# Waiting only for counters that have moved: the entry waits of a fully serialised eight-core kernel

## What is computed

```python
def bit_linear(x, w):
    xn = (x - mu) / jnp.sqrt(var + 1e-05)              # over a whole batch element
    wq = jnp.clip(jnp.round(w * ws), -1.0, 1.0) / ws   # ternary weights
    xq = jnp.clip(jnp.round(xn * xs), -128.0, 127.0) / xs
    return xq @ wq.T

def ode_func(z, Wqkv, Wo_o, a_o, b_o):                 # called 8 times
    h = dyn_tanh(z, a_o, b_o)
    q, k, v = split(bit_linear(h, Wqkv))               # 16 heads of 64
    attn = softmax(q @ k.T * scale)
    return bit_linear(attn @ v, Wo_o)

xn = layernorm(x)
h = xn + retention(xn)
s = ode_block(h)                                       # 2 steps of 4 ode_func
g = silu(ffn(xn))                                      # 1024 -> 4096 -> 1024
return x + s * g
```

## Time and profile before

| | before |
|---|---|
| median of 3 runs | 43872.15 us (43852.11 to 43897.67) |
| profiled execution, its time | 43859.97 us |
| profiled execution, span of the slowest core | 43858.4 us |
| spans of the 8 cores | 43794.8 to 43858.4 us |
| mean granted TensorE clock, by core | 0.612 to 0.613 |
| instructions of the slowest core | 223059 |
| PE / DVE / ACT / POOL busy | 12665.3 / 7484.7 / 10799.9 / 834.4 us |

### The profile page before, as it was taken

The page is one execution under the profiler, slowest core; times in us unless marked ns, Lnnn a source line. Parts: engine busy times, 40 slices in busy tenths (PEclk is TensorE's granted clock), DMA queues, the critical chain, the costliest instruction groups (busy, mean ns, idle before and its releaser), DMA issues.

```text
span 43858.4 us, 223059 instructions; the slowest of 8 cores (43794.8 to 43858.4 us)
## 1 busy us (share of the span) xinstructions
PE 12665.3 (29%) x42533; PEld 4313.3 (10%) x42816; DVE 7484.7 (17%) x15282; ACT 10799.9 (25%) x8116; POOL 834.4 (2%) x1572
## 2 busy tenths in 40 slices
PE   0000012222321442343244144214414422432441
PEld 0000000000100110111011011101101101110110
DVE  2222220001222002101200310220030021012002
ACT  0000020000022332333333333233333333332331
POOL 1111100000000000000000000000000000000000
PEclk9999985555555555555555555555555555555555
DMA  1111111111000000000000000000000000000001
GB/s 39 40 39 39 39 37 47 44 44 42 11 4 26 2 3 12 5 2 3 14 3 3 14 3 3 19 20 2 3 14 3 2 10 7 3 2 14 3 3 60
DMA packets 702215, 749.02 MB, mean 17 GB/s; under 512 B 309250, under 2 KB 526851, under 8 KB 700931
## 3 DMA queue, kind: packets, MB, share of 16 engines
q1 hardware_dynamic: 635908, 615.10, 4.7%
q0 software_dynamic: 65024, 119.64, 0.8%
HBM read 614.82 MB, written 119.54 MB: 17 GB/s over the span
## 4 chain that ended last, share of the span: by engine, by line
PE 29%; issue 21%; DVE 17%; ACT 15%; DMA 12%; SPq 3%; DVEq 1%; POOL 1%; ACTq 1%; POOLq 0%
ACT psb L1326 9%; PE pC L1306 9%; PE pA L1318 9%; DMA wdb<-wTdown 2%; PE pA L1242 2%; PE pC L1414 1%; PE pA L1222 1%; PE pA L762 1%; DMA xt<-z_h 1%; PE pA L678 1%; DVE q_r L336 1%; ACT q_t L323 1%; PE pT L215 1%; DMA xt<-wdown 1%; DVE yfm L1337 1%
## 5 line engine op out<-in xcount | busy, mean ns | idle before, releaser
L1306 PE MATMUL pC<-psb,vsb 128*65 128x512 bf16 x8192 | 3864.2, 625 | 7381.4 <-ACT psb L1326 7381.4
L1326 ACT ACT_TABLE_LOAD x2048 | 2627.6, 1283 | 9912.7 <-PE pA L1318 9912.7
L1318 PE MATMUL pA<-qsb,ksb 64*128 64x512 bf16 x8192 | 3847.5, 623 | 850.1 <-DVE hy L1358 803.5
L1326 ACT ACTIVATE psb<-pA,negCb 128x2048 bf16<-128x2048 f32 x2048 | 4028.4, 1967 | 24.6
L1337 DVE CAST yfm<-pC 65x512 bf16<-65x512 f32 x512 | 351.8, 687 | 15287.9 <-PE pC L1306 15287.9
L1306 PEld LDWEIGHTS pC<-psb,vsb 128*65 128x65 bf16 x8192 | 1109.5, 160 | 10196.3 <-issue 10196.3
L565 ACT ACT_TABLE_LOAD x16 | 20.5, 1283 | 5797.6 <-DVE st L560 5797.6
L512 PE MATMUL pT<-midn,q_xq 128*128 128x128 bf16 x1344 | 196.6, 301 | 4032.2 <-DVE q_xq L504 4032.2
L215 PE MATMUL pT<-midn,q_xq 128*128 128x128 bf16 x2432 | 307.6, 306 | 3465.1 <-ACT q_xq L344 3465.1
L239 PE MATMUL pD<-s_csts,st 128*1 128x1 f32 x36 | 3.4, 163 | 4448.5 <-DVE st L234 4448.5
L1318 PEld LDWEIGHTS pA<-qsb,ksb 64*128 64x128 bf16 x8192 | 865.2, 126 | 3296.6 <-issue 3296.6
(11 more groups left out here) (252 smaller groups left out, 15045.3 us busy)
## 6 DMA issues: line engine op xcount, KB each, us to landing
xt<-z_h SPq DMA_DIRECT2D x176, 512.0 KB
wgb<-wTgate SPq DMA_DIRECT2D x512, 128.0 KB
wub<-wTup SPq DMA_DIRECT2D x512, 128.0 KB
wdb<-wTdown SPq DMA_DIRECT2D x512, 128.0 KB
xt<-wgate SPq DMA_DIRECT2D x128, 256.0 KB
xt<-wup SPq DMA_DIRECT2D x128, 256.0 KB
xt<-wdown SPq DMA_DIRECT2D x128, 256.0 KB
xt<-wqkv SPq DMA_DIRECT2D x96, 256.0 KB
```

What stands on the lines that cost most here:

```text
L1306: self.t.inc(te.matmul(self.pC1[0:65, :], vsb2[:, mt, h01 * 65:h01 * 65 + 65], psb2[:, m4 * 512:(m4 + 1) * 512], start=(mt == 0), stop=(mt ...
L1318: self.t.inc(te.matmul(self.pA[:, m4 * 512:(m4 + 1) * 512], ksb2[bp:bp + 64, mt * 128:(mt + 1) * 128], qsb2[bp:bp + 64, ncc * 512:(ncc + 1 ...
L1326: self.s.inc(se.activation(out=psb2[:, 0:2048], in_=self.pA[:, 0:2048], func=ACT.Exp, scale=0.125, bias=self.negCb[:, h01:h01 + 1]))
```

## The change

`SerialBlock` now remembers, for each engine, the value of each counter that the engine's last entry wait asked for. At a function's entry it waits only on those of the five counters whose `n` has grown since then. The waits inside the functions, among them explicit calls of `vwait_all`, stay as they are and aren't remembered.

```diff
     def __init__(self, bld):
         self._bld = bld
+        self._seen = {}
 
     def _wrap(self, name):
         def deco(fn):
             real = getattr(self._bld.block, name)
+            seen = self._seen.setdefault(name, {})
+            b = self._bld
             @real
             def _(eng):
-                self._bld.vwait_all(eng)
+                for ch in (b.ld, b.qg, b.t, b.v, b.s):
+                    if seen.get(id(ch), -1) < ch.n:
+                        eng.wait_ge(ch.h, ch.n)
+                        seen[id(ch)] = ch.n
                 fn(eng)
         return deco
```

## The result

The change makes the kernel faster: 42871.38 us (median of 8 runs, 42864.88 to 42891.64) against 43871.61 us (8 runs of before beside it). The ratio is 0.9772, 95% interval 0.9762 to 0.9783. Forecast were 42840 us and a range of 42740 to 43020.

A forecast was written before the change was run, and what follows sets the result against it. Functions run one after another, so time between them counts: 1003 us of waits plus 30 of instruction fetch make 1033, and 43872 - 1033 gives 42840 us, range 42,740 to 43,020.

The forecast's parts named there:

- the projections: V, Q and K projections, 64 head pairs: seven PE and eight DVE waits behind a release go, saving 82 us.
- all else: Token tiles starting with a load, weight scales, functions behind barriers and the last stage: saving 90 us.
- A wait costs its spacing behind the release: At function entries, only removed waits behind the counter satisfied last save their spacing, 0.050 to 0.105 us each by engine.
- PE's 0.105 us: Price of one PE entry wait behind the release, derived from gaps before matmuls and transposes: 0.105 us.
- Rival 2: PE waits give back only their recorded 51 ns, so the time would be 43,075 us; chance 0.07.
- rival 1: Entry waits are hidden in idle time after all, so the time would stay 43,872 us; chance 0.03.
- 1003 us by the walk: All functions' removed entry waits behind a release, counted one by one with actual starts: 1003 us saved.
- Instruction fetch, 30 us: Stalls at multiples of 128 instructions on an engine: fewer instructions save 30 us, between 0 and 80.
- rival 3: TensorE's clock falls in the projections, losing their fast stretches: slower, about 44,120 us; chance 0.02.
- Rival 4: TensorE's clock rises in the attention's matmul bursts, 1.8 us less each, 2048 times: about 39,150 us; chance 0.02.
- What the changed profile would show: Signs: 46,403 waits, attention round 7.25 us, gaps 0.24 and 0.25 us, busy times within 0.5%, "issue" near 20%.

The follow-up runs named there:

- the two added waits: Kernel before with two never-blocking waits added at each function's entry: ahead of the five 43774.56 us, behind them 46580.65 us, against 43739.12.
- the sorted five: Kernel before with all five entry waits kept but sorted so the counter raised last in the program comes last: 42104.19 us, ratio 0.9627.
- every wait once: The change plus sorted order, also leaving out waits inside functions already made for that value or a higher one: 40993.15 us, ratio 0.9371.

## Why the prediction was right, point by point

**The functions run strictly one after another, so a removed nanosecond between two of them counts.** Right. Stage by stage, the terms come out within 14 us, except in the projections and in "all else".

**A wait costs its spacing behind the release and next to nothing ahead of it.** Shown, by the two added waits (35 against 2,842 us) and by the sorted five (1,635 us for no wait removed).

**PE's 0.105 us, derived from three gaps.** Right: 0.56 to 0.24 us in the down loop, 0.35 to 0.24 at the transposes, 413 us for PE alone. Rival 2, with 0.051, has fallen; so has rival 1, that the waits are hidden anyway.

**1003 us by the walk.** 1000 us between the medians. The agreement is partly luck: the projections gave 25 us instead of 82, and the token tiles and load-started functions in "all else" gave some 40 more than their term, which the rounded sum of terms had set low.

**Instruction fetch, 30 us.** Not shown. 34,542 more instructions cost 35 us where 15 were due to position, and 45,172 fewer at the same order gave nothing (1,634 against 1,635 us). The best values put the term between 0 and some 20 us, but the intervals of these ratios leave room for the 30. They fit the Trainium skill (Runtime: NRT & Kernel Launch, Instruction fetch mechanics, "mostly hidden") better than the prediction's weighing against it: single gaps of 0.4 us are real, but in the sum nothing was seen of them.

**The step that was mis-sized: the projections, 82 us, and with it the clause that shorter gaps cost no clock.** This is rival 3 in small. I had given it 0.02 as an event that takes all fast stretches or none; it took part of one. In the changed kernel a K burst looks like this in the chain:

```profile
28421.91 2.30 DVE qsb L1256
28424.21 0.24 issue
28424.45 8.76 PE pA L1248 x32
```

and in two windows over it (length, busy us of each engine, PEclk, DMA share, GB/s):

```profile
28424.40:28427.80 3.40, 3.35 (x8) 1.17 (x9) 0.00 (x0) 0.00 (x0) 0.00 (x0) 0.51 0.02 5
28427.90:28433.00 5.10, 5.10 (x25) 2.21 (x23) 0.00 (x0) 0.00 (x0) 0.00 (x0) 1.00 0.00 0
```

Its first 8 matmuls take 3.35 us at the lower level (1.2 GHz; the window's granted clock is 0.51), the rest run at 1.00 (2.4 GHz). That happens in 59 to 64 of 64 K bursts on the eight cores, before the change in 12 to 20. The mean K matmul says the same in the groups by line, before and in the changed kernel:

```profile
L1242 PE MATMUL pA<-hqT,wkb 128*128 128x512 bf16 x1984 | 476.2, 395 | 193.2 <-DVE qsb L1250 189.8
```

```profile
L1248 PE MATMUL pA<-hqT,wkb 128*128 128x512 bf16 x2048 | 550.2, 436 | 179.2 <-DVE qsb L1256 179.2
```

It is 436 ns against 395. The mean K burst grew from about 7.5 to 8.6 us, 64 times: some 70 us, which covers the difference of 57 between term and measurement. Ahead of the result the Trainium skill's rule (TensorE: Matmul & The Clock Gate, What's actually happening), by which idleness makes the clock fall, was read as a reason that shorter gaps do no harm. The trace disagrees with this reading: less idle time went with more time at the lower level.

That the V groups' spacing brings most of this about is shown by the kernels with the change in V alone and in Q and K alone. How it does can be read in the traces' records of the granted clock. The level changes only at the points of an even grid: all but a few in a thousand of the stretches at one level are whole multiples of one length, before and after. Where no change happens at a point, its place is counted on from the last change. Which level a K burst gets goes by where in the grid it starts. Before, 111 of the 512 K bursts of all cores start less than 0.95 us behind a point, and all 111 are slow; of the 401 that start later behind one, 395 run wholly at the upper level. With the change in V alone the bursts that do so start at 0.96 us or more, as before, but the median start has moved from 1.27 to 0.74 us behind a point. With Q and K alone the median is 0.90 us, and the first such burst starts at 0.78. So a saving of a fraction of a microsecond moves K to the other side of that bound. It isn't a matter of more or less idleness: of 64 K bursts of the slowest core 16 are slow before, 54 with two waits behind, 40 with the change on PE alone, 63 after, 63 with every wait once. What sets the bound stays open.

**Rival 4**, a faster clock in the attention, didn't happen: the round lost its 0.055 us and no more.

**What the changed profile would show.** The count of waits, the two ACTq pieces, the round and both gaps came as forecast. Two signs did not: PE's busy time rose by 1.1% instead of staying within 0.5%, partly by the missing records and partly by the clock in K, and "issue" fell to 9% instead of near 20%.

## What to carry to other kernels

Of several waits in a row, only those behind the one that is released last cost anything, and each costs the distance at which the sequencer issues them (here 0.05 to 0.105 us), not its recorded duration (17 to 51 ns). So put the counter that is raised last at the end, and leave out repeats of a wait that the engine has already made; in a serialised program of 17,000 functions that was worth 6.3%, and almost all of the change under study is contained in it. Where a short shift moves matmuls that follow a rise of the granted clock, expect some tens of microseconds to come or go, and look at the clock of the bursts before believing a small gain.

## What the runs showed that was not expected

- The granted clock at the K projection depends on timing 10 to 20 us earlier: the same 32 matmuls take 7.07 us in most cases before and 8.4 to 8.8 us in most cases after, with less idle time ahead of them.
- A table load on ACT is cut into two pieces of the chain when waits of the next function are executed beside it, and 1.2 us of it are then labelled "issue".
- 34,542 additional instructions, 15% more, made a difference of 35 us in 43,739 when hardly any stood behind a release.
